# Recurrence scores for two heads at a time on row strips of TensorE, with keys masked once and a causal mask over the diagonal blocks only

## The reference, cut to what matters

```python
qh, kh, vh = (split(q), split(k), split(v))
log_f_cum = ...                                  # running sum of log_sigmoid(forget gate)
log_fg = jnp.where(ltr, fg_mat[:, :, 1:, 1:], -jnp.inf)
log_D = log_fg + jnp.transpose(ig, (0, 1, 3, 2))
max_log_D = jnp.max(log_D, axis=-1, keepdims=True)
D = jnp.exp(log_D - max_log_D)
qk = jnp.einsum('bhsd,bhtd->bhst', qh, kh) / jnp.sqrt(jnp.asarray(dh, q.dtype))
C = qk * D
normalizer = jnp.maximum(jnp.abs(C.sum(-1, keepdims=True)), jnp.exp(-max_log_D))
Cn = C / (normalizer + EPS)
h = jnp.einsum('bhst,bhtd->bhsd', Cn, vh)
...                                              # h is then centred and scaled per head
```

## Time and profile before

| | before |
|---|---|
| time, median of 3 runs | 1420.99 us (1420.01 to 1421.34) |
| span of the profiled execution (first to last instruction) | 1414.4 us |
| median less that span | 6.6 us |
| PE, DVE, ACT, POOL busy, share of the span | 82%, 51%, 34%, 29% |

### The profile page before, as it was taken

One profiled execution on the slowest core, in us unless ns is written; L12 is line 12 of the kernel. 1 busy time (PEld: TensorE's weight loads), 2 busy tenths in 40 slices (PEclk: granted clock), 3 DMA queues, 4 the chain that ended last, 5 costly groups with the idle time before them and its releaser, 6 DMA issues. The chain is left out here.

```text
span 1414.4 us, 20117 instructions
## 1 busy us (share of the span) xinstructions
PE 1156.9 (82%) x6280; PEld 883.5 (62%) x6280; DVE 723.0 (51%) x1850; ACT 480.2 (34%) x1324; POOL 411.8 (29%) x468
## 2 busy tenths in 40 slices
PE   5999999999660999086999999869946849999994
PEld 3777777778530887033777778737723537777773
DVE  5777787863440233220555561137864426566564
ACT  0333333341200232022555551125531234454442
POOL 3555555523535122640000000101141032342211
PEclk9999999999865899578999999979976879999997
DMA  9300000000012897214000000000001041112000
GB/s 334 146 23 22 22 22 22 11 1 1 1 37 89 267 299 252 83 43 144 10 14 12 12 1 1 19 5 2 0 1 36 1 134 45 45 52 83 0 1 30
DMA packets 72976, 82.16 MB, mean 58 GB/s; under 512 B 8417, under 2 KB 63527, under 8 KB 72912
## 3 DMA queue, kind: packets, MB, share of 16 engines
q1 hardware_dynamic: 59200, 50.94, 11.9%
q0 software_dynamic: 5632, 15.73, 3.2%
q10 hardware_dynamic: 8080, 14.69, 2.8%
HBM read 60.22 MB, written 22.02 MB: 58 GB/s over the span
## 5 line engine op out<-in xcount | busy, mean ns | idle before, releaser
L346 PE MATMUL a_proj_ps<-xT,a_w 128*128 128x512 f32 x256 | 121.8, 610 | 9.7 <-DMA a_w<-in_L_attn_Wv_dram 9.5
L248 ACT ACTIVATE a_probs<-a_score_ps,a_nmax 128x128 f32<-128x128 f32 x128 | 47.1, 368 | 207.3 <-DVE a_nmax L241 207.3
L221 PEld LDWEIGHTS a_turn_ps<-ident,a_probs 128*128 128x128 f32 x384 | 47.9, 142 | 65.7 <-DVE a_probs L259 32.8
L438 POOL TENSOR_TENSOR a_qk<-a_by_cos,a_by_sin 128x512 f32<-128x512 f32 x64 | 85.2, 1330 | 5.0
L104 POOL TENSOR_SCALAR ln_d_var<-ln_d_ssq 128x1 f32<-128x1 f32 x8 | 1.5, 192 | 283.6 <-ACT ln_d_sq L98 283.4
L221 PE MATMUL a_turn_ps<-ident,a_probs 128*128 128x128 f32 x384 | 65.0, 279 | 22.0 <-DVE a_probs L259 22.0
L346 PEld LDWEIGHTS a_proj_ps<-xT,a_w 128*128 128x128 f32 x256 | 47.3, 195 | 55.3 <-issue 49.8
L265 ACT ACTIVATE a_probsT<-a_turn_ps 128x384 f32<-128x384 f32 x128 | 62.5, 488 | 54.4 <-PE a_turn_ps L221 54.4
L240 DVE TENSOR_REDUCE a_nmax<-a_score_ps 128x1 f32<-128x128 f32 x128 | 36.6, 286 | 76.3 <-PE a_score_ps L214 75.7
L340 PEld LDWEIGHTS a_proj_ps<-a_w,xT 128*128 128x128 f32 x512 | 63.7, 196 | 15.5 <-issue 7.4
L434 POOL TENSOR_TENSOR a_by_sin<-a_swapped,sin_q 128x512 f32<-128x512 f32 x32 | 40.7, 1271 | 112.1 <-DVE a_swapped L394 112.1
(11 more groups left out here) (373 smaller groups left out, 3140.9 us busy)
## 6 DMA issues: line engine op xcount, KB each, us to landing
slots<-zeros ACTq DMA_DIRECT2D x4, 2048.0 KB, 16.6
e_rows<-slots SPq DMA_DIRECT2D x32, 256.0 KB, 4.2
e_w<-in_L_ffn_w_dram SPq DMA_DIRECT2D x32, 256.0 KB, 3.8
out_slots<-e_out POOLq DMA_DIRECT2D x32, 256.0 KB, 4.8
e_w<-in_L_ffn_w_dram SPq DMA_DIRECT2D x32, 128.0 KB, 3.8
m_up_w<-in_up_dram SPq DMA_DIRECT2D x8, 512.0 KB, 3.9
a_w<-in_L_attn_Wq_dram SPq DMA_DIRECT2D x16, 128.0 KB, 2.2
a_w<-in_L_attn_Wk_dram SPq DMA_DIRECT2D x16, 128.0 KB, 2.3
```

Source lines behind the costliest of these rows:

```text
L221: last = pe.transpose(self.turn_ps[:, r, j * P:(j + 1) * P], self.probs[:, r, j * P:(j + 1) * P], self.k.ident[:, :])
L346: last = pe.matmul(proj_ps[:, c % 2, :], w[:, par, 0 if what == "q" else 1, kc, :], k.xT[:, kc, half * HALF:(half + 1) * HALF], start=kc = ...
L438: pool.tensor_tensor(qk[:, par, 0 if what == "q" else 1, half * HALF:(half + 1) * HALF], by_cos[:, r, :], by_sin[:, r, :], ALU.add).then_i ...
```

## The change

Six things change in `layer1_lstm`, and one instruction group is added to `layer1_gates`:

1. The keys are masked once, ahead of the stage: POOL forms `k.keys` (two copies of `cT`, for even and for odd heads: the 16 rows of the other head of each 32-row strip are zero) in four instructions of 128 x 1024. DVE's `keys`, once a head, is gone.
2. `products` now does two heads at a time. Each matmul takes only the 32 rows (`STRIP`) in which its head lies, at `tile_position=(strip, 0)`, and the two heads of a pair lie on different strips: `ORDER` takes the heads of a group as 0, 2, 1, 3.
3. The mask matmul covers the two diagonal blocks only (2 x 128 columns in place of 384).
4. `l_qk_ps` has four slots in place of two, and `l_z_ps` two in place of four (`ZRING = 2`).
5. PE emits, for each pair n, n+1: `exponents` of n+2 and n+3, `products` of the pair n+2, and then the `mix` or the `turn`.
6. The hardware loop over batches is written out, and `l_g_b` gets two slots. ACT's order stays as it was.

```diff
@@ layer1_gates, POOL
                 pool.memset(k.nM_rows[:, :, :], 0.0).then_inc(v_zero, 1)
+                pool.wait_ge(k.ctx1_in, k.ctx1_loads)
+                for half in range(2):
+                    for c in range(DC):
+                        pool.tensor_scalar(k.keys[:, half, c, :], k.cT[:, c, :], k.head_of[:, half:half + 1], 1.0,
+                                           ALU.mult, ALU.mult).then_inc(k.keyed, 1)
@@ layer1_lstm
     RING = 4
+    ZRING = 2
+    STRIP = 2 * LW
+    HEADS_C = P // LW
+    ORDER = [GROUP * g + i for g in range(GROUPS_B) for i in (0, 2, 1, 3)]
...
-        z_ps = m.ps("l_z_ps", [P, RING, 512])
-        qk_ps = m.ps("l_qk_ps", [P, 2, 512])
+        z_ps = m.ps("l_z_ps", [P, ZRING, 512])
+        qk_ps = m.ps("l_qk_ps", [P, RING, 512])
...
-                def exponents(b, h):
-                    at_least(pe, exped, LH * b + h - RING + 1)
-                    pe.matmul(z_ps[:, h % RING, 0:CAUSAL], k.ident_bf[:, :], k.after_bf[:, :], start=True, stop=False)
+                def exponents(n):
+                    b, h = n // LH, ORDER[n % LH]
+                    at_least(pe, exped, n - ZRING + 1)
+                    z = z_ps[:, n % ZRING, :]
+                    pe.matmul(z.rearrange("p (a s) -> p a s", a=2)[:, :, 0:P], k.ident_bf[:, :],
+                              k.after_bf[:, :].rearrange("p (a s) -> p a s", a=2), start=True, stop=False,
+                              skip_group_check=True)
+                    pe.matmul(z[:, 0:CAUSAL], k.sel[:, h, :], k.nM_rows[:, b, :], start=False, stop=True,
+                              skip_group_check=True).then_inc(z_done, 1)
+                def products(n):
+                    at_least(pe, C_done, n + 1 - RING + 1)
+                    b = n // LH
+                    for keys_at, x_at, to in ((b * S, slice(b * S, (b + 1) * S), slice(0, S)),
+                                              (b * S + P, slice(b * S + P, (b + 1) * S), slice(S, CAUSAL))):
+                        for u in (n, n + 1):
+                            h = ORDER[u % LH]
+                            c, strip = h // HEADS_C, h % HEADS_C // 2 * STRIP
+                            rows = slice(strip, strip + STRIP)
+                            last = pe.matmul(qk_ps[:, u % RING, to], k.keys[rows, h % 2, c, keys_at:keys_at + P],
+                                             k.xT[rows, c, x_at], start=True, stop=True, tile_position=(strip, 0))
+                    last.then_inc(qk_done, 1)
...
+                exponents(0)
+                exponents(1)
+                products(0)
+                for n in range(0, LH * B, 2):
+                    exponents(n + 2)
+                    exponents(n + 3)
+                    products(n + 2)
+                    G = n // GROUP - 1
+                    if G >= 0:
+                        if n % GROUP == 0:
+                            mix(G)
+                        else:
+                            turn(G)
```

More of the change, by code:

```diff
@@ L1359, in layer1_lstm @@
         STEPS = TAKE + SPREAD + SCALE
[L1361 to L1366, removed]
         with nc.Block() as block:
@@ L1391, in products @@
[L1391 to L1405, removed]
+                pe.wait_ge(k.keyed, 2 * DC)
+                def exponents(n):
+                    if n >= LH * B:
+                        return
+                    b, h = n // LH, ORDER[n % LH]
[6 more added lines that the diff above has]
+                              skip_group_check=True).then_inc(z_done, 1)
@@ L1406, in mix @@
+                def mix(G):
+                    b, g = divmod(G, GROUPS_B)
                     pe.wait_ge(C_done, GROUP * (G + 1))
@@ L1422, in turn @@
                     for q in range(QT):
-                        last = pe.transpose(turn_ps[:, q * P:(q + 1) * P], hT[:, g % 2, q * P:(q + 1) * P],
+                        last = pe.transpose(turn_ps[:, q * P:(q + 1) * P], hT[:, G % 2, q * P:(q + 1) * P],
                                             k.ident[:, :])
                     last.then_inc(turned, 1)
[L1427 to L1442, removed]
@@ L1447, in _, with keep_hT @@
+                mix(B * GROUPS_B - 1)
+                turn(B * GROUPS_B - 1)
             @block.scalar
             def _(act):
-                def keep_hT(b, g):
-                    G = GROUPS_B * b + g
+                def keep_hT(G):
                     act.wait_ge(mixed, G + 1)
                     at_least(act, turned, G - 1)
-                    act.activation(hT[:, g % 2, :], hT_ps[:, 0:S], ACT.Copy).then_inc(hT_kept, 1)
-                def keep_raw(b, g):
-                    G = GROUPS_B * b + g
+                    act.activation(hT[:, G % 2, :], hT_ps[:, 0:S], ACT.Copy).then_inc(hT_kept, 1)
@@ L1457, in keep_raw @@
+                def keep_raw(G):
+                    b, g = divmod(G, GROUPS_B)
                     act.wait_ge(turned, G + 1)
@@ L1462, in keep_raw @@
                                    ).then_inc(raw_kept, 1)
[L1464 to L1482, removed]
+                for n in range(LH * B):
+                    b, h = n // LH, ORDER[n % LH]
+                    if n % LH == 0:
+                        act.wait_ge(batch_ready, b + 1)
+                    act.wait_ge(z_done, n + 1)
+                    at_least(act, C_done, n - RING + 1)
+                    act.activation(dec[:, n % RING, 0:S], z_ps[:, n % ZRING, 0:S], ACT.Exp,
+                                   bias=g_b[:, b % 2, 0, h:h + 1])
+                    act.activation(dec[:, n % RING, S:CAUSAL], z_ps[:, n % ZRING, S:CAUSAL], ACT.Exp,
+                                   bias=g_b[:, b % 2, 1, h:h + 1]).then_inc(exped, 1)
+                    G = n // GROUP - 1
+                    if G >= 0:
+                        if n % GROUP == 1:
+                            keep_hT(G)
+                        elif n % GROUP == 3:
+                            keep_raw(G)
+                keep_hT(B * GROUPS_B - 1)
+                keep_raw(B * GROUPS_B - 1)
             @block.vector
@@ L1497, in fetch @@
                 def fetch(b):
[L1498 to L1503, removed]
+                    at_least(dve, exped, LH * (b - 1))
+                    dve.tensor_copy(g_b[:, b % 2], k.g_tok[:, :, ROWS * b:ROWS * b + LH]).then_inc(batch_ready, 1)
                 def take(b):
@@ L1539, in _ @@
                 values(0)
[L1540 to L1562, removed]
-                                spread(b - 1)
-                            elif h == 15:
-                                scale(b - 1)
-                    if not last:
+                for n in range(LH * B):
+                    b, i = divmod(n, LH)
+                    h = ORDER[i]
+                    dve.wait_ge(exped, n + 1)
+                    dve.wait_ge(qk_done, n // 2 + 1)
+                    if n % GROUP == 0:
+                        at_least(dve, mixed, n // GROUP - 1)
+                    dve.tensor_tensor(C[:, h % (2 * GROUP), :], dec[:, n % RING, :], qk_ps[:, n % RING, 0:CAUSAL],
+                                      ALU.mult).then_inc(C_done, 1)
+                    if b > 0:
+                        if i == 2:
+                            dve.wait_ge(mixed, GROUPS_B * b)
+                            values(b)
+                        elif i == 4:
+                            take(b - 1)
+                        elif i == 7:
+                            spread(b - 1)
+                        elif i == 15:
+                            scale(b - 1)
+                    if i == 8 and b + 1 < B:
                         fetch(b + 1)
-                batches(dve, emit)
                 take(B - 1)
```

34 lines of the change are left out of this document (14 added, 20 removed).

## The result

The changed kernel takes 1483.5 us (median of 4 runs, 1480.1 to 1485.2) against 1420.5 us for the kernel before beside it: a ratio of 1.046, 95% interval 1.043 to 1.049. The span of the profiled execution went from 1414.4 to 1478.2 us, 63.8 us more. It is slower, as forecast, but by three times as much (63 us against 21), and outside the range of 1430 to 1478.

The account below looks back on a forecast made before the run. PE set the pace before; the two-slot ring was to bind after, at 7.25 us a period against 5.62: +22.8 over 14 periods, less 1 at the start, span 1436.2, plus 6.6 around it: 1442 us, range 1430 to 1478.

Parts of the forecast that it names:

- The ring: Two exponent slots make PE and ACT wait in turn: 5.75 us plus twice the products' time, 7.25 us a period.
- The rival that the ring would not bind: Exponentials run ahead and PE's issue bounds the stage: period 4.0 us, time 1398; chance 0.07.
- The clock: PE's granted clock in the stage: expected at 1.00 from the first group on, so nothing added to the sum.
- My comparison by busy share: PE's expected busy half of the period, set against stretches with clock 0.99 (4.89 of 10 us) and 0.50 (7.18 of 16.8).
- The rival of the low clock: PE at 1.2 GHz for part or all of the stage: up to +47 us, time 1455 to 1489; chance 0.16.
- the change of shape: PE's switch of tile shape: 0.09 us, once before and once behind the products, 0.18 in each half period.
- the way from `mix` to `keep_hT`: From the start of PE's `mix` to the start of ACT's copy: 0.93 us of the period.
- The 6.6 us around the span: Time outside the profiled span, added to the forecast span of 1436.2 us to give 1442.8.
- The products of a pair: Two heads' products on different row strips of PE: 0.75 us, between 0.65 at full overlap and 1.30 without.
- POOL's four key instructions: Masked keys formed on POOL before the stage: expected to cost nothing, at most 9.6 us if all before the barrier.
- The start: DVE's first `l_C` can begin up to 2 us earlier without the keys; 1 us taken off the time.
- The last step from group 14 to 15: The stretch from the last two `mix` on keeps its chain, so it was to cost nothing more.

Follow-up runs that it names:

- the warm start: Changed kernel plus 20 matmuls of no use (128x512 bf16) on PE ahead of the stage, while PE waits for DMAs: 1470.2 us.
- The third slot: Changed kernel with three slots for the exponents in place of two, copy and transpose sharing a bank: 1469.3 us.
- the order alone: Changed kernel with PE's `mix` or `turn` issued ahead of the step's exponents and products: 1396.0 us in one run, 1396.9 in three rounds.
- full rows: Changed kernel with products over all 128 rows of the array, so a pair's two heads can't overlap: 1449.0 us.

## Why the prediction was right or wrong

**The ring: right, and to size.** The chain of `mix`, copy, exponentials, exponents, products, `turn` is in the trace step by step. At full clock its period is 7.24 us against 7.25 worked out, and its two halves are 3.85 and 3.39 against 3.13 + 0.75 = 3.88 and 2.62 + 0.75 = 3.37. The time there is 1432, with the warm start, against the 1442 that I gave. The third slot shortened it as it should, and cutting it by the order took the period to 4.06. The rival that the ring would not bind (period near 4.0, 1398) is what the order alone gave, at 1396; I had seen no place for the overlap in the changed order, and there is none in it.

**The clock: the step that failed.** The sum kept the clock at 1.00 and so put the clock's term at nothing; it measured 40 us. I gave the fall of the clock 0.16, with two reasons against it: "by that measure the new stage is above 0.5; and the stage starts with dense work". Both were true and neither helped. The stage started with 10.00 of 10.00 us busy, and PE was busy for 79% of it, at 0.50. The records count a matmul of 32 rows as busy like one of 128 (the products' records have a median of 374 ns in the run of the order alone and of 379 in that with full rows), and the clock does not go by them: the same order with full rows got 1.00 at 68% busy, with 32 rows on one strip it stayed at 0.50 at 84%. My comparison by busy share, from stretches whose matmuls all had 128 rows or several strips at once, did not carry over to row strips. Nor is it the strips by themselves. With the ring's gaps and full rows the clock stayed at 1.00, with strips and no ring it did so too, and with strips, ring and full-row matmuls in the gaps as well; with strips and the bare ring it fell from 1.00 after 955.2, or never rose. In these runs it took both. The Trainium skill (TensorE: Matmul & The Clock Gate, The HAM clock gate) says that the clock follows how busy PE has been; here a PE that was always busy by the profile was not given it, and the measurement decides.

**How the loss divides.** Of the 63.0 us, the ring makes 14 x (7.24 - 5.62) = 22.7, and the clock 14 x (10.12 - 7.24) = 40.3. The rival of the low clock was priced at 47 and 1489; measured, 40.3 and 1483.5. Not all that I had doubled did double: the change of shape went from 0.09 to 0.13, and the way from `mix` to `keep_hT` from 0.93 to 1.58.

**Smaller terms.** The 6.6 us around the span were too many: in the runs here an execution's time is 1.8 to 2.4 above its span, so the 6.6 held some 4 us of difference between one execution and another, and a span of 1436.2 would have been 1438. The products of a pair were taken as 0.75 and are 0.76 (overlap on strips: right). POOL's four key instructions take 4.42 us, from 916.13 to 920.55, less than half of the 9.6 taken from two-input rows; they held up nothing, as said:

```profile
916.13 4.42 POOL L1308 TENSOR_SCALAR keys<-cT,head_of 128x1024 f32<-128x1024 f32 x4
```

The start gained nothing: from the first exponents to group 0's `mix` it takes 11.02 us (945.00 to 956.02) in place of 10.65, and I had taken 1 off. In the run with a warm start it is 6.30 (944.52 to 950.82), so it is the low clock that holds it. The last step from group 14 to 15 went from 3.20 to 3.85 us, at half clock; I had it at nothing.

**What stays open.** Why the clock needs both, the strips and the ring, to stay down. Whether the gaps themselves count, or how little full-row work the stage then has in a given time, no run parts. And whether a dense stage of strips alone would hold the clock: in the new order a good part of PE's time is other matmuls, and no run had strips only.

## What to carry to other kernels

Before you give an engine less to do, walk once round every ring that its output slots and its consumer's queue close, and add it up: here it was 7.25 us against a period of 5.62, and the cure was not a slot but to put the work that the consumer waits for ahead of the work that waits for the consumer. In a stage that waits, matmuls on few rows can cost the clock that all the others run on: check the granted clock of the stage, not the busy time, and compare the same stage with full rows. Where PE is idle anyway, full-row matmuls of no use can pay: the ring ran 48 us faster with them, those ahead of the stage included.

## What the runs showed of the hardware

- Busy by the records and still at 1.2 GHz: 32-row f32 products with bf16 full-row exponents, 10.00 of 10.00 us. The same with 128-row products went to 2.4 GHz within 4 us. With the ring's gaps out of the way the 32-row stage had 2.4 GHz too, for 72 us when it started there.
- Two f32 matmuls of 32 rows and 128 columns of weights on different row strips do overlap: at half clock the eight records of a pair take 1.65 us on two strips and 2.92 on one. At full clock they take 0.92, where 128 rows take 1.47 in the run with full rows:

```profile
959.66 1.47 PE L1409 MATMUL l_qk_ps<-xT,keys 128*128 128x256 f32 x8
```

- POOL multiplies 128x1024 f32 by a column and a constant in 1.12 us, less than half of its 2.40 for two tensors of that width.
